# DLRM forward: the last pair's odd fields gathered by POOL, shared copies for two pairs, and a spare gather at the start

## The reference

```python
x = relu(dense @ W0 + b0); x = relu(x @ W1 + b1); dense_out = relu(x @ W2 + b2)
emb = vmap(lambda t, idx: t[idx], in_axes=(0, 1), out_axes=1)(tables, sparse)   # 2048 x 26 x 64
gram = einsum('bid,bjd->bij', emb, emb)
features = concatenate([dense_out, gram[:, TRIU_I, TRIU_J]], axis=1)            # 64 + 325 columns
y = features @ Wt + bt                                                          # 2048 x 256
```

## Time and profile before

| | |
|---|---|
| Time of three runs | 544.02 us median (543.76 to 544.22) |
| Profiled execution | 543.01 us |
| Its span | 541.2 us |
| Busy: POOL, PE, DVE, ACT | 376.6, 303.3, 258.0, 8.8 us |
| Mean granted TensorE clock | 0.700 of full speed |
| Gathers of POOL | 374 and 24 |
| Rows fetched by hand | 1152 by SP, 1152 by ACT |

### The profile page before, as it was taken

The page is one execution under the profiler, slowest core; times in us unless marked ns, Lnnn a source line. Parts: engine busy times, 40 slices in busy tenths (PEclk is TensorE's granted clock), DMA queues, the critical chain, the costliest instruction groups (busy, mean ns, idle before and its releaser), DMA issues.

```text
span 541.2 us, 9582 instructions
## 1 busy us (share of the span) xinstructions
PE 303.3 (56%) x1752; PEld 240.6 (44%) x1752; DVE 258.0 (48%) x672; ACT 8.8 (2%) x21; POOL 376.6 (70%) x405
## 2 busy tenths in 40 slices
PE   2814761667766667678581733619163281824667
PEld 1514541546555556457461622417052260614555
DVE  5254533445575653836465450715536163551823
ACT  2000000000000000000000000000000000000012
POOL 5777777777777777777777777777777777777100
PEclk9965575777597957777677575856657575565889
DMA  7222224222222223232222222322222222221100
GB/s 108 29 29 31 31 47 90 38 29 38 29 29 38 28 30 38 30 37 28 38 28 35 32 37 30 38 29 30 37 29 39 28 38 28 31 36 28 20 11 11
DMA packets 25850, 18.81 MB, mean 35 GB/s; under 512 B 15575, under 2 KB 19385, under 8 KB 25772
## 3 DMA queue, kind: packets, MB, share of 16 engines
q0 software_dynamic: 12736, 13.07, 16.7%
q1 hardware_dynamic: 6612, 2.52, 5.3%
q10 hardware_dynamic: 6442, 2.61, 5.0%
HBM read 15.25 MB, written 2.10 MB: 32 GB/s over the span
## 4 chain that ended last, share of the span: by engine, by line
ACTq 52%; issue 13%; SPq 10%; DMA 9%; PE 8%; DVE 7%; DVEq 0%
ACTq L248 40%; ACTq L242 11%; SPq L248 6%; DMA by_hand<-in_L_rec_tables_dram 4%; DVE gram L232 4%; DMA w_tri<-in_L_rec_Wt_dram 3%; PE gram_ps L642 3%; PE mlp_ps L569 2%; PE mlp_ps L658 2%; SPq L242 2%; DMA w_gram<-w_tri 1%; SPq L281 1%; DVE h L413 1%; DMA raw_idx<-n_r_sparse_features_dram 1%; DVE embT L209 1%
## 5 line engine op out<-in xcount | busy, mean ns | idle before, releaser
L317 POOL DMA_INDIRECT emb<-in_L_rec_tables_dram,row_idx x374 | 353.1, 944 | 117.6 <-issue 113.9
L232 DVE COPY gram<-gram_ps 32x96 f32<-32x96 f32 x496 | 161.1, 325 | 97.0 <-PE gram_ps L642 85.6
L621 PE MATMUL rowsT_ps<-ident,emb 128*128 128x128 f32 x187 | 37.1, 333 | 134.8 <-DMA emb<-in_L_rec_tables_dram,row_idx 127.5
L642 PE MATMUL gram_ps<-embT 64*128 64x100 f32 x1024 | 91.3, 345 | 27.5 <-DVE gram L232 14.4
L642 PEld LDWEIGHTS gram_ps<-embT 64*128 64x128 f32 x1024 | 85.3, 254 | 37.0 <-issue 37.0
L621 PEld LDWEIGHTS rowsT_ps<-ident,emb 128*128 128x128 f32 x187 | 24.6, 166 | 146.4 <-issue 145.7
L209 DVE COPY embT<-rowsT_ps 128x512 f32<-128x512 f32 (+1 forms) x60 | 47.7, 851 | 85.5 <-PE rowsT_ps L621 85.1
L658 PE MATMUL mlp_ps<-w_gram,gram 128*128 128x256 f32 x224 | 70.1, 481 | 4.4 <-DVE gram L232 4.3
L569 PE MATMUL mlp_ps<-h,w_sb 128*128 128x256 f32 x128 | 48.7, 561 | 32.6 <-DVE h L413 32.6
L658 PEld LDWEIGHTS mlp_ps<-w_gram,gram 128*128 128x128 f32 x224 | 57.5, 258 | 17.8 <-DVE gram L232 5.2
L569 PEld LDWEIGHTS mlp_ps<-h,w_sb 128*128 128x128 f32 x128 | 37.1, 297 | 45.4 <-DVE h L413 37.0
(11 more groups left out here) (39 smaller groups left out, 45.4 us busy)
## 6 DMA issues: line engine op xcount, KB each, us to landing
by_hand<-in_L_rec_tables_dram SPq DMA_DIRECT2D x1152, 0.2 KB
by_hand<-in_L_rec_tables_dram ACTq DMA_DIRECT2D x1152, 0.2 KB
emb<-in_L_rec_tables_dram,row_idx POOLq DMA_INDIRECT x374, 4.8
out_dram<-out_sb ACTq DMA_DIRECT2D x16, 128.0 KB, 14.1
w_gram<-w_tri SPq DMA_DIRECT2D x3, 192.0 KB
w_sb<-in_L_rec_W_dram SPq DMA_DIRECT2D x1, 512.0 KB
emb<-in_L_rec_tables_dram,last_idx POOLq DMA_INDIRECT x24, 3.5
raw_idx<-n_r_sparse_features_dram SPq DMA_DIRECT2D x2, 182.0 KB, 4.2
```

The costliest lines, as they stand in the source:

```text
L232: last = copy(by_quad[FP * g:FP * (g + 1), t0:NS, :, half * HG:(half + 1) * HG, s], gram_ps[FP * s:FP * (s + 1), :, :, src:src + SQ * (NS ...
L317: nc.gpsimd.indirect_dma_start(emb[:, m % PR, k, u, :], None, tables_v[:, :], bass.IndirectOffsetOnAxis(ap=row_idx[:, 2 * m + u, k:k + 1], ...
L621: last = nc.tensor.transpose(rowsT_ps[c % 2][:, k - ks.start, :, :], rows.rearrange("p u e -> p (u e)"), ident[:, :])
L642: last = nc.tensor.matmul(gram_ps[:, u, a, 0:SQ * (F - 1)], samples.rearrange("p s f -> p (s f)"), samples[:, :, 1:F], start=True, stop=True)
```

## The change

Pair 15 leaves `BY_HAND`, so that eight pairs are left there. Its step `k` = 12 is fetched by two gathers of POOL, which come first of the last pair's gathers; the entry `None` moves to the front of `LAST_CHUNKS`. In PE's program all three chunks of half 0 and its products now stand ahead of `top(14)`, and in DVE's the copies of those products ahead of `out_evac(14)`. The copies of pair 14 are shared between DVE and ACT as those of pair 15 are (`SHARED`). ACT stores pairs 13 and 14 between these copies. POOL gets one more gather, of row 0 on all partitions into a buffer that nobody reads, ahead of its wait for the first indices; DVE sets its index to zero in a small memset.

```diff
-    BY_HAND = [2, 4, 5, 7, 9, 10, 12, 14, 15]
+    BY_HAND = [2, 4, 5, 7, 9, 10, 12, 14]
...
-    LAST_CHUNKS = [(0, 0, 4), (0, 4, LK), None, (1, 0, 4), (1, 4, 5), (1, 5, LK)]
+    LAST_CHUNKS = [None, (0, 0, 4), (0, 4, LK), (1, 0, 4), (1, 4, 5), (1, 5, LK)]
...
+    SHARED = range(LAST_PAIR - 1, NP)
...
+            pool.wait_ge(row_zero_set, 1)
+            nc.gpsimd.indirect_dma_start(spare_rows[:, :], None, tables_v[:, :],
+                                         bass.IndirectOffsetOnAxis(ap=row_zero[:, 0:1], axis=0)
+                                         ).then_inc(spare_rows_in, 16)
             pool.wait_ge(idx_ready, 1)
...
                 if chunk is None:
+                    for u in range(2):
+                        nc.gpsimd.indirect_dma_start(
+                            emb[:, LAST_PAIR % PR, HAND_K, u, :], None, tables_v[:, :],
+                            bass.IndirectOffsetOnAxis(ap=row_idx[:, 2 * LAST_PAIR + u, HAND_K:HAND_K + 1], axis=0),
+                        ).then_inc(last_rows_in[i], 16)
                     continue
...
             nc.vector.memset(ident[:, :], 0.0).then_inc(zeros_set, 1)
+            nc.vector.memset(row_zero[:, :], 0).then_inc(row_zero_set, 1)
...
-                if m < LAST_PAIR:
+                if m not in SHARED:
                     gram_evac(nc.vector.tensor_copy, BLOCKS, m, half).then_inc(gram_ready, 1)
...
+            gram_blocks(LAST_PAIR, 0)
             out_evac(LAST_PAIR - 1)
-            gram_blocks(LAST_PAIR, 0)
...
-            act.wait_ge(top_in_psum[LAST_PAIR % 2], LAST_PAIR // 2)
-            for half in range(2):
-                act.wait_ge(gram_in_psum, LAST_PAIR * 2 + half + 1)
-                gram_evac(nc.scalar.copy, ACT_BLOCKS, LAST_PAIR, half).then_inc(gram_tail_act, 1)
+            for m in SHARED:
+                act.wait_ge(top_in_psum[m % 2], m // 2)
+                for half in range(2):
+                    act.wait_ge(gram_in_psum, m * 2 + half + 1)
+                    gram_evac(nc.scalar.copy, ACT_BLOCKS, m, half).then_inc(gram_tail_act, 1)
+                    if half == 0 and m == LAST_PAIR:
+                        store(m - 1)
+                if m < LAST_PAIR:
+                    store(m - 1)
             store(LAST_PAIR)
...
-                    for u in range(2):
-                        pe.wait_ge(by_hand_in[BY_HAND.index(LAST_PAIR)][u], 16 * P)
-                    rows = [by_hand[:, BY_HAND.index(LAST_PAIR), :, :]]
+                    pe.wait_ge(last_rows_in[i], 16 * 2)
+                    rows = [emb[:, LAST_PAIR % PR, HAND_K, :, :]]
...
-            last_transposes(0)
-            last_transposes(1)
+            for i in range(HALF_DONE[0]):
+                last_transposes(i)
+            gram_products(LAST_PAIR, 0)
             top(LAST_PAIR - 1)
-            last_transposes(2)
-            gram_products(LAST_PAIR, 0)
             last_transposes(3)
```

More of the change, by code:

```diff
@@ L122, in bass_dlrm_forward @@
         row_idx = sb("row_idx", [P, NU, NK], u32)
+        row_zero = sb("row_zero", [P, 1], u32)
+        spare_rows = sb("spare_rows", [P, EMB])
         last_raw = sb("last_raw", [P, 4, F], i32)
@@ L162, in bass_dlrm_forward @@
         later_ready = sem("later_ready")
+        row_zero_set = sem("row_zero_set")
+        spare_rows_in = sem("spare_rows_in")
         last_idx_in = sem("last_idx_in")
@@ L339, in _ @@
                         ).then_inc(last_rows_in[i], 16)
+            pool.wait_ge(spare_rows_in, 16)
         @block.vector
@@ L524, in _ @@
                 fetch_rows(act, 1, m, c0, c0 + LOADED)
-            for done in range(LAST_PAIR):
+            for done in range(SHARED.start - 1):
                 if done * 7 // 3 + 7 >= len(pieces):
                     store(done)
-            act.wait_ge(top_in_psum[LAST_PAIR % 2], LAST_PAIR // 2)
-            for half in range(2):
-                act.wait_ge(gram_in_psum, LAST_PAIR * 2 + half + 1)
-                gram_evac(nc.scalar.copy, ACT_BLOCKS, LAST_PAIR, half).then_inc(gram_tail_act, 1)
+            for m in SHARED:
[7 more added lines that the diff above has]
+                    store(m - 1)
             store(LAST_PAIR)
@@ L623, in transposes, with blocks_out @@
                     last.then_inc(rowsT_in_psum[c], 1)
-            def gram_products(m, half):
[L628 to L632, removed]
+            def blocks_out(count):
+                first = 2 * SHARED.start
+                wait_if_any(pe, gram_ready, min(count, first))
+                if count > first:
+                    pe.wait_ge(gram_tail_dve, count - first)
+                    pe.wait_ge(gram_tail_act, count - first)
+            def gram_products(m, half):
+                blocks_out(2 * m + half)
                 if m == LAST_PAIR:
@@ L650, in top @@
                 nc.tensor.matmul(mlp_ps[q][:, 0:NO], h2[:, m // 2, q * P:(q + 1) * P], wd_sb[:, :], start=True, stop=False)
[L652 to L656, removed]
+                blocks_out(2 * m + 2)
                 for t in range(NS):
```

## The result

| | before | after |
|---|---|---|
| Median of four runs each, same chip | 543.89 us (543.68 to 544.22) | 528.33 us (526.34 to 529.84) |
| Ratio | | 0.9711, 95% interval 0.9677 to 0.9745 |
| Profiled execution, its span | 543.01, 541.2 us | 528.75, 527.0 us |

The gain is 15.6 us, where 20.6 was forecast, and the time lies 4.9 us above the predicted 523.4: 0.2 us inside the upper end of the range. The runs of the changed kernel spread over 3.5 us, those of before over 0.5; two of the changed kernel's four lie above the range.

What follows compares the result with a forecast made beforehand. POOL's gathers bound 92% of the span, then a wait for hand-fetched rows. POOL ends 1.8 us later, but the last transposes follow it 22.4 us closer: 544.02 - 20.6 = 523.4 us, range 520.9 to 528.5.

Steps and rivals of the forecast that it cites:

- a small backlog being drained, not a latency: DMA queue at the kernel's end: hand-fetched rows feed a backlog some 20 us deep, draining at 4 GB/s.
- lag-stays rival: End of the gather queue: gathers themselves fill it, the last lands 20.0 us late, time 539.2 us; chance 8%.
- POOL's two gathers: POOL's gather sequence: two more gathers cost 2 x 1.249 = 2.50 us, fully on the path; last gather ends at 504.2.
- the other two rivals: Spare gather delays POOL's start, 525.4 us, 5%; or lag grows with 26 last-pair gathers, up to 545.1 us, 3%.
- a slower drain: Backlog after pair 14's hand-fetched rows: drain leaves those rows some 5 us later still, setting the range's 528.5 us end.
- within 2 us of 507.7: Sign of being right: PE's last transposes come that close to the forecast landing of POOL's last gather.
- the earliest end: Kernel's end: last gather lands 3.4 us after POOL's 504.2, then 12.07 us of unchanged work, so no span under 519.8.
- Does PE hold it up?: PE's work from pair 14's rows at 479.5 to the last transposes at 509.3; span 521.4, middle taken as 520.6.
- nothing that PE or DVE do in the loop can matter: Main loop: POOL issues gathers without a break for 92% of the span, so other engines' work there is hidden.
- the same rows would add up to 3 us: PE's last steps: a low clock through them would lengthen the end by up to that much.
- The forecast of the drain: Pair 14's last gathered rows: hand-fetched rows in at 467.4, then 12.1 us of queued gathers, landing 479.5; bounds 475.1 to 492.4.
- I count 0.62, less 0.06 for a semaphore: POOL's start: spare gather pays the first-gather gap in idle time; with 0.16 from a shorter gather, 0.72 us saved.

## Why the prediction was right, and where its size went wrong

**Right: the bound, and what removes it.** The lag is "a small backlog being drained, not a latency", and the hand-fetched rows feed it: fetching the same rows 3 to 5% slower halves the backlog, dropping pair 14's rows empties it by 440, and dropping pair 15's empties it by the end. The lag-stays rival falls (longest landing 2.6 us after 490). With it falls the outcome by the Trainium skill's page "DMA: Bandwidth & Descriptors", section "Issuing engines are not separate DMA queues": by that rule the move to POOL would have given 539, and it gave 528.33 (526.30 by itself). In this kernel 128 rows fetched one by one loaded the DMAs otherwise than 128 rows of one gather. The page of the kernel before counts for SP's queue

```profile
q1 hardware_dynamic: 6612, 2.52, 5.3%
```

and that of the changed one 6356, 256 packets less for 128 rows less, on ACT's queue as well; a gather of 128 rows has 32. So pair 15's 256 odd rows were 512 packets by hand and are 64 by POOL. The Trainium skill's page "DMA: Bandwidth & Descriptors", section "Why a DMA increments its semaphore by 16 and not by 1", by which a one-row DMA could sit on a single engine, would agree; no row here shows the load of one engine, so that a single engine is what filled up stays open.

**Right: POOL's two gathers, and the other two rivals.** The last gather ends at 504.65 (504.2 forecast). The spare gather does not delay the start, and the kernel is not slower than before.

**Luck: the range.** The median lies 0.2 us inside it, and the upper end, 528.5, was put there for a slower drain, which did not come. Of the signs named, the last transposes "within 2 us of 507.7" failed: they came at 515.13. The lower end adds 1.5 us to its span of 519.4, where the forecast adds 2.8 to 520.6; that decided nothing.

**Wrong: the earliest end.** "So the span cannot end before 507.7 + 12.07 = 519.8": the profiled execution with 16 offsets at a time has a span of 517.9. The sum counted the last landing from the end of the gather's row, where the view counts it from the start, 0.94 us earlier, and took 3.4 us for it, where 2.5 were measured.

**Wrong in size: "Does PE hold it up?".** That step began its sum at pair 14's third chunk, "From 479.5 this leads to 492.9", with the rows' arrival as the only thing PE waits for. It left out that pair 13's last chunk still lands in the full backlog, so that PE is already behind when pair 14's rows come. The trace of the kernel before had it, in PE's transposes of pair 13's last step, DVE's copies of pair 13's second half and its first copy of pair 14:

```profile
462.39 0.45 PE L621 MATMUL rowsT_ps<-ident,emb 128*128 128x128 f32 x1 [1.73 <-DMA emb<-in_L_rec_tables_dram,row_idx]
...
475.00 5.35 DVE L232 COPY gram<-gram_ps 32x96 f32<-32x96 f32 x16 [1.62 <-PE gram_ps L642]
...
480.38 1.03 DVE L209 COPY embT<-rowsT_ps 128x512 f32<-128x512 f32 x1
```

PE's third chunk needs the buffer that this last copy empties at 481.4, whenever the rows come. For the same reason "nothing that PE or DVE do in the loop can matter" did not hold for the loop's last two pairs. The sum beside the profile:

| | forecast | profile after | difference |
|---|---|---|---|
| Pair 14's third chunk transposed | 479.5 | 482.18 | +2.7 |
| From there to the transposes behind `top(14)` | 25.7 | 29.03 | +3.3 |
| From those to the last transposes | 4.14 | 3.92 | -0.2 |
| The last transposes by this sum | 509.3 | 515.13 | +5.8 |

The sum went to the middle between POOL's 507.7 and this 509.3, which gives away another 0.8, so the miss at the last transposes is 6.6 us of 508.5; the 12.07 behind them came out at 11.87, and the span 6.4 us above 520.6. The first line is the wait for DVE's copies of pair 13: in the run that shares them the wait is 2.7 us shorter. The second is the low clock: products of half 0 in 3.74 us instead of 2.5, and in the timeline `top(13)`'s matmuls in 5.23 and `top(14)`'s in 5.46 us, where the sum had 4.24 for each. The prediction named this ("the same rows would add up to 3 us") and did not take it. That it counts in full is again a matter of PE being late: with 16 offsets at a time `top(14)` is hardly faster, 4.92 us, and yet the last transposes stand right behind POOL.

The forecast of the drain, 479.5 for pair 14's rows, was too late, not too early: no gather issued after 472 lands later than 3.4 us, and with 16 offsets at a time PE transposes that chunk at 473.80. PE's own delay hid this error.

**Wrong: the spare gather.** "I count 0.62, less 0.06 for a semaphore": the gap between indices and first gather went from 0.92 to 0.79 us only. It is what this wait costs, warm or not. The 0.16 of the shorter gather came. With and without it the time is the same within the intervals (0.9616 and 0.9617). The load of about 6 us that the Trainium skill's page "GPSIMD Engine Reference", section "Instruction dispatch", states for a first call is seen nowhere: the first gather of all takes 1.10 us.

**Sharing and order.** The prediction gave them worth only once the wait for rows is gone. With the wait still there they cost 4.1 us. That they are worth something once it is gone is not shown: 1.3 us is seen of pair 14's sharing, inside the intervals, and the kernel without sharing, new order and spare gather is as fast as the changed one (0.9695 and 0.9711).

Not tried: the slower fetching with pair 15 still fetched by hand, what the chain from 462 would take at the higher clock throughout, and whether the wider spread of the changed kernel's runs comes from the clock in that chain.

## What to carry to other kernels

When a backlog is removed, follow it forward from the last thing that fed it: the first consumer behind it that is still late can start a chain of work that outlasts the gain. A feeder that is a few per cent too fast builds a queue over a whole run, so look at how the longest landing grows before removing its work; on top of the change, slowing it slightly brought as much here (521.3 us) as taking one more pair away from it (523.0), within the intervals. And where several edits come together, run the main one alone: here it carried all of the gain.

## What the runs showed of the hardware

- The backlog grows over the run: the longest landing of the changed kernel is 7.6 us at 50:100, 7.1 at 150:200, 14.0 at 250:300, 17.0 at 350:400 and 20.8 at 440:472, while the shortest stays at 3.3 to 3.4. Row DMAs 3 to 5% slower halve it.
- With no row DMAs beside them gathers land in 2.4 to 2.8 us (490:506 of the changed kernel, 440:472 with seven pairs by hand); beside them, in the windows above, the best was 3.3.
- The first gather after POOL's wait for a semaphore starts 0.79 us behind it even when a gather has gone before; gathers without a wait follow each other by 0.30.
- A smaller largest piece for a 256-byte row DMA left the number of packets as it was, and nops between DMA issues on SP left their pace as it was.
- Loading 16 offsets at a time instead of 32 cost 5% of SP's pace late in the run, 0.402 us for a row instead of 0.384, and 3.4% over its last 896 rows.
- The granted clock was full through spare matmuls (3.62 us) and the wait of 2.22 us behind them, and at the lower level (0.51) from the transposes at 482.67 on, through the products behind them.
